# The last layer in one stage: scan over chunks 0 to 4, then 5 to 7, with the gating of the first five chunks between units of the second part

## What is computed

```
# state-space mixer, u of shape (b, l, d), n = 16 states for every channel
A = -exp(log_A)
dt = softplus(u @ W_dt.T + b_dt + dt_bias)
Bt = (u @ W_B.T + b_B).reshape(b, l, d, n)
Ct = (u @ W_C.T + b_C).reshape(b, l, d, n)
A_bar = exp(dt[..., None] * A)
x_in = (A_bar - 1) / A * Bt * u[..., None]
h_t = A_bar_t * h_(t-1) + x_in_t          # along the sequence
y_t = sum_n(Ct_t * h_t) + D_skip * u_t
x = layernorm(u + y)
# mixture
h = gelu(x @ wg1 + bg1); probs = softmax(h @ wg2 + bg2)[:, :20]
top_vals, top_idx = top_k(probs, 2)
out = sum over the two experts e of top_val * (x @ We[e] + be[e])
x = layernorm(x + out)
```

## Time and profile before

| | us |
|---|---|
| median of 3 runs | 2651.47 |
| the three runs | 2647.59, 2654.21, 2651.47 |
| span of the profiled execution | 2646.7 |
| busy in the span: PE / DVE / ACT / POOL | 2472.2 / 1964.7 / 1382.1 / 1110.7 |
| scan: first to last matmul start | 1610.0 to 2339.4 |
| mixture: first pair's matmul | 2415.0 |

### The profile page before, as it was taken

One profiled execution on the slowest core, in us unless ns is written; L12 is line 12 of the kernel. 1 busy time (PEld: TensorE's weight loads), 2 busy tenths in 40 slices (PEclk: granted clock), 3 DMA queues, 4 the chain that ended last, 5 costly groups with the idle time before them and its releaser, 6 DMA issues. The chain is left out here.

```text
span 2646.7 us, 43896 instructions
## 1 busy us (share of the span) xinstructions
PE 2472.2 (93%) x15059; PEld 1552.6 (59%) x15059; DVE 1964.7 (74%) x4037; ACT 1382.1 (52%) x2469; POOL 1110.7 (42%) x1092
## 2 busy tenths in 40 slices
PE   7999999999999999899999997999999999977992
PEld 4433333333333333467777775888888888855772
DVE  3777777777777774266676657999999999975256
ACT  3466666666666666444455535655555555543320
POOL 3522222222222221110000004999989898944454
PEclk9999999999999999999999998999999999987996
DMA  8633333323333321100000000000000000024785
GB/s 244 174 70 71 82 58 58 58 58 58 58 58 69 70 64 66 54 16 17 16 24 25 9 17 8 13 12 12 12 12 12 12 12 12 4 86 130 238 282 162
DMA packets 109601, 166.41 MB, mean 63 GB/s; under 512 B 15876, under 2 KB 74296, under 8 KB 106232
## 3 DMA queue, kind: packets, MB, share of 16 engines
q1 hardware_dynamic: 99064, 143.24, 21.5%
q0 software_dynamic: 6144, 16.79, 2.0%
q10 hardware_dynamic: 4224, 4.19, 0.5%
HBM read 97.66 MB, written 62.01 MB: 60 GB/s over the span
## 5 line engine op out<-in xcount | busy, mean ns | idle before, releaser
L644 ACT ACTIVATE ssm_in_dt<-att_s 128x512 f32<-128x512 f32 (+3 forms) x1280 | 610.0, 535 | 346.9 <-PE att_s L541 182.7
L733 DVE TENSOR_REDUCE att_partmax<-att_s 128x1 f32<-128x512 f32 x768 | 494.3, 686 | 109.8 <-PE att_s L515 66.4
L541 PE MATMUL att_s<-att_qs,att_ks 49*128 49x512 f32 (+3 forms) x1280 | 433.9, 419 | 16.1 <-ACT ssm_in_dt L644 13.8
L515 PE MATMUL att_s<-att_ks,att_qs 49*128 49x512 f32 (+3 forms) x1280 | 434.5, 424 | 4.9 <-DVE att_qs L723 4.7
L541 PEld LDWEIGHTS att_s<-att_qs,att_ks 49*128 49x128 f32 x1280 | 207.4, 185 | 380.3 <-ACT ssm_in_dt L644 307.6
L1797 POOL TENSOR_TENSOR ssm_cc<-ssm_cc,ssm_h 128x512 f32<-128x512 f32 x256 | 334.9, 1308 | 75.7 <-DVE ssm_h L1858 73.8
L432 POOL TENSOR_SCALAR_AFFINE_SELECT ssm_in_dt<-ssm_in_dt 128x256 f32<-128x256 f32 x256 | 104.6, 409 | 621.5 <-ACT ssm_in_dt L644 562.8
L584 PE MATMUL att_o_ps<-ssm_in_dt,att_vst 128*32 128x512 f32 (+3 forms) x2560 | 340.6, 542 | 5.3 <-ACT ssm_in_dt L644 5.3
L1812 POOL TENSOR_TENSOR ssm_out_z<-ssm_out_z,ssm_cc 128x512 f32<-128x512 f32 x256 | 340.4, 1330 | 0.1
L1737 ACT ACTIVATE ssm_cc<-ssm_c_ps,ssm_cur 128x512 f32<-128x512 f32 x256 | 199.0, 777 | 211.8 <-PE ssm_c_ps L1686 211.5
L736 DVE CUSTOM_DVE_ANT_0 att_hid<-att_s,att_hidden 128x512 bf16<-128x512 f32 (+3 forms) x512 | 238.8, 487 | 94.6 <-PE att_s L515 93.7
(11 more groups left out here) (324 smaller groups left out, 4183.7 us busy)
## 6 DMA issues: line engine op xcount, KB each, us to landing
qk_halves<-ssm_in_dt SPq DMA_DIRECT2D x64, 256.0 KB
moe_sorted<-att_hidden SPq DMA_DIRECT2D x31, 512.0 KB, 9.4
moe_rows<-moe_sorted SPq DMA_DIRECT2D x62, 256.0 KB
moe_answers<-moe_mixed SPq DMA_DIRECT2D x62, 256.0 KB
att_far<-bias_tables SPq DMA_DIRECT2D x96, 136.0 KB, 8.5
att_stage_q<-qk_halves SPq DMA_DIRECT2D x96, 128.0 KB, 4.4
att_stage_k<-qk_halves SPq DMA_DIRECT2D x96, 128.0 KB, 5.9
ssm_raw<-in_w_bc SPq DMA_DIRECT2D x30, 256.0 KB, 2.6
```

The source lines that it names most:

```text
L515: mm = nc.tensor.matmul(s1[:, S1_BANK[at], 0:hi - lo], qs[p % 3][half(b, ROWS), I * P:(I + 1) * P], ks[p % 3][half(b, ROWS), lo:hi], start ...
L541: mm = nc.tensor.matmul(s2[:, turn % RING, 0:hi - lo], ks[p % 3][half(b, ROWS), J * P:(J + 1) * P], qs[p % 3][half(b, ROWS), lo:hi], start ...
L644: nc.scalar.activation(prob[:, b, step % 2, x * CH + lo:(x + 1) * CH], s2[:, turn % RING, 0:CH - lo], ACT.Exp, scale=1.0 / HD).then_inc(s2 ...
L733: nc.vector.tensor_reduce(most, piece, AX, ALU.max).then_inc(s1_read, 1)
```

## The change

Both stages become one, `phase_scan`; `phase_mixture` is empty. (The first layer's stage only writes its step sizes chunk by chunk in memory; same instructions.)

1. The units are written out, with no loop on the engines. They run over 32 blocks (n, m) for chunks 0 to 4 (160 units, part one), then over the 32 blocks again for chunks 5 to 7 (96 units, part two). The state at the end of chunk 4 is kept for each block (`carry`), since chunk 5 goes on from it.
2. The rounded weights are made once, in part one, every 5 units. SyncE stores them to DRAM (`scan_halves`, 512 KB a block) and loads them back in part two, one block for 3 units. VectorE's remainder now reads the raw weights from a copy in PSUM.
3. `hi` and `lo` hold 5 chunks; chunks 5 to 7 are rounded over 0 to 2 at the end of part one.
4. PSUM: 3 banks of decays instead of 2, 2 for B instead of 4, 2 for C, and one spare bank, through which all the gating of chunks 0 to 4 goes.
5. The gating of chunks 0 to 4 is put between units of part two at fixed unit numbers: turn c starts at unit 160 + 1 + 7c. Normalising and copying out of transposes move from VectorE to ScalarE for these chunks. GpSimd's 16 scatters of group 0 stand at every second unit from unit 213 to 243.
6. The experts' weights are loaded in part two, over `u` and `dt` of chunks 0 to 4.
7. After the last unit come the pairs at once; `turn_z`, `turn_x`, `hide` and `logits` of chunks 5 to 7 stand among pairs 0 to 14, `count(2)` at pair 18 (before: 14), the exponentials of group 2 at pair 17 (before: 11). The 24 scatters of group 1 follow GpSimd's last unit.

```diff
+PART_CHUNKS = ((0, 1, 2, 3, 4), (5, 6, 7))
...
+def gate(turn):
+
+    return SPLIT + 1 + 7 * turn
...
-            with eng.Fori(0, N - 1) as n:
-                for m in range(KT):
-                    eng.wait_ge(w_ready, KT * n + m + 1)
-                    eng.dma_start(raw[:, m], t.w_bc[ds(n + 1, 1), m].rearrange("a p k c -> (a p) k c")).then_inc(raw_loaded[m], 16)
...
+            def load_halves(b):
+                if b < KT:
+                    eng.wait_ge(halves_stored[b], 16 * N)
+                    eng.wait_ge(c_ready, SPLIT - (KT - 1 - b) * HELD)
+                else:
+                    eng.wait_ge(c_ready, first_unit(b - 1, 1))
+                eng.dma_start(halves[b % KT][:].rearrange("p a k c -> p (a k c)").bitcast(F32), t.halves_bc[b]).then_inc(halves_loaded[b % KT], 16)
...
+                for out_ps, read, ready, ring, col in ((b_ps[:, g % B_RING], b_read, b_ready, B_RING, slice(0, P)),
+                                                       (c_ps[:, g % C_RING], c_read, c_ready, C_RING, slice(P, 2 * P))):
+                    after(eng, read, g - ring + 1)
...
+            for g in range(UNITS):
+                states(g)
+                for c in range(HELD):
+                    for s in range(2):
+                        if g == gate(c) + s:
+                            turn_z(c, s)
+                    for k in range(KT):
+                        if g == gate(c + 2) + 2 + k:
+                            turn_x(c, k)
+                    if g == gate(c + 2) + 4:
+                        hide(c)
+                    if g == gate(c + 3) + 6:
+                        logits(c)
+                if g == gate(6) + 5:
+                    count(0)
+                if g == gate(9) + 5:
+                    count(1)
...
+                nc.scalar.copy(spare.rearrange("p (k c) -> p k c", k=KT), src).then_inc(raw_copied, 1)
...
+                    if g == gate(c + 1):
+                        spread(c)
+                    for j in range(TPC):
+                        if g == gate(c + 1) + (2, 3, 4, 6)[j]:
+                            normalise(c, j)
...
+            for g in range(UNITS):
+                if g + 1 < UNITS:
+                    multiply(g + 1)
+                add(g)
+                for n in range(GROUP_TILES[0]):
+                    for k in range(2):
+                        if g == gate(7) + 3 + 4 * n + 2 * k:
+                            scatter(0, n, k)
...
+                nc.vector.tensor_tensor(halves[m][:, 1], spare.rearrange("p (k c) -> p k c", k=KT), halves[m][:, 0].bitcast(F32),
+                                        ALU.subtract).then_inc(w_ready, 1)
```

More of the change, by code:

```diff
@@ L1003, in tokens @@
         def tokens(c):
-            return dt[:, :, c * CH:(c + 1) * CH]
+            return steps[:, c]
         def expn_at(c):
@@ L1955, with unit, last_unit @@
 STORE_AT = [COMBINED[TPC * q + TPC + 1] + 2 for q in range(EARLY - 1)]
-def phase_mixture(nc, t):
+BLOCKS = N * KT
+PART_CHUNKS = ((0, 1, 2, 3, 4), (5, 6, 7))
+HELD = len(PART_CHUNKS[0])
+SPLIT = BLOCKS * HELD
+UNITS = BLOCKS * NCH
+def unit(g):
+    part = 0 if g < SPLIT else 1
+    chunks = PART_CHUNKS[part]
+    block, at = divmod(g - SPLIT * part, len(chunks))
+    return block // KT, block % KT, chunks[at], block, part, at
+def last_unit(ch):
+    part = 0 if ch in PART_CHUNKS[0] else 1
+    chunks = PART_CHUNKS[part]
+    return SPLIT * part + (BLOCKS - 1) * len(chunks) + chunks.index(ch)
@@ new lines, in decayed, with scan @@
+            def decayed(g):
+                eng.wait_ge(a_ready, g + 1)
+                eng.wait_ge(b_read, g + 1)
+                nc.vector.scalar_tensor_tensor(out=inp[:, g % 2], in0=a_ps[:, g % A_RING], scalar=1.0, in1=inp[:, g % 2],
+                                               op0=ALU.subtract, op1=ALU.mult).then_inc(inp_ready, 1)
+            def scan(g):
+                n, m, ch, b = unit(g)[0:4]
+                after(eng, multiplied, g - H_RING + 1)
+                kept = len([x for x in range(max(0, g - H_RING + 1)) if unit(x)[2] == HELD - 1])
+                if 0 < kept and unit(g - H_RING)[2] == HELD - 1:
+                    eng.wait_ge(carried, kept)
+                if g == SPLIT:
+                    eng.wait_ge(carried, BLOCKS)
+                eng.wait_ge(inp_ready, g + 1)
+                if ch % (S // CH) == 0:
+                    begin = 0.0
+                elif ch == HELD:
+                    begin = carry[:, b:b + 1]
+                else:
+                    begin = h[:, (g - 1) % H_RING, CH - 1:CH]
+                nc.vector.tensor_tensor_scan(h[:, g % H_RING], a_ps[:, g % A_RING], inp[:, g % 2], begin, ALU.mult, ALU.add).then_inc(h_ready, 1)
@@ L2414, in means, with moments, variance @@
+            def moments(c, s):
+                eng.wait_ge(z_copied, 2 * c + s + 1)
+                for j in (2 * s, 2 * s + 1):
+                    ins = nc.vector.bn_stats(stats[:, j], x3[:, TPC * c + j])
+                step.go(ins)
+            def variance(c):
+                step.wait()
+                for j in range(TPC):
+                    ins = nc.vector.bn_aggr(mv[:, TPC * c + j], stats[:, j])
                 ins.then_inc(var_ready, 1)
-            def normalise(c):
+                eng.wait_ge(var_ready, c + 1)
@@ L2528, in _ @@
[L2528 to L2540 removed]
+            pre = t.last_pre
+            step(nc.vector.memset(one[:], 1.0))
+            round_w(0)
+            round_lo(0)
+            nc.vector.scalar_tensor_tensor(out=t.last_expn, in0=pre, scalar=-1.0, in1=pre, op0=ALU.mult, op1=ALU.min).then_inc(last_abs, 1)
@@ L2545, in _ @@
+            whole_normalise(7)
             read_x(7)
-            choose(2)
-            settle(2)
+            read_logits(6)
+            read_logits(7)
+            shift(2)
+            share(2)
+            for q in range(3):
+                largest(2, q)
+            for q in range(3):
+                whose(2, q)
+            chosen(2)
+            joined(2)
+            spots(2)
+            places(2)
+            passes(2)
             list_tiles(2)
```

1254 lines of the change are left out of this document (656 added, 598 removed).

## The result

| | before | changed |
|---|---|---|
| median (8 runs each) | 2649.81 us | 2660.82 us |
| lowest to highest | 2640.92 to 2654.21 | 2659.49 to 2668.29 |
| ratio, 95% interval | | 1.0048 [1.0038, 1.0059] |
| span of the profiled execution | 2646.7 | 2658.8 |

What follows compares the result with a forecast made beforehand. TensorE was taken to bound scan and pairs, with a latency-bound 75 us stretch between. Terms -68 + 26 + 13 - 6 + 2 + 3 + 8 gave -22 us, a median of 2629 us; 8 in 10 within 2603 to 2656.

Steps and rivals of the forecast that it cites:

- Pairs: +8: Pairs' stage: transposes of chunks 5 to 7, waits for chunk 5's chain and for count(2) add 8 us.
- The stretch before the pairs, -68: Between the scan's last matmul and the first pair: 75.5 us shrink to a 7 us wait for GpSimd, gaining 68.
- Part one: Scan of chunks 0 to 4: units stay at 2.80 us, VectorE's remainders fit under TensorE, cost 0.
- Start, -6: First seven units, 32.1 us before: three of six remainders go and the softplus moves behind, 6 us less.
- Part two, 295 to 312 us forecast: Scan of chunks 5 to 7 with the gating between its units: 295 to 312 us long instead of 269.
- the small waits: TensorE's small waits on the gating chain in part two, such as logits behind group 0's places: 3 us more.
- +38: The whole scan, both parts with the start: forecast to take 38 us longer than before.
- The +13: Part two: VectorE's added operations wait 0.6 us each for GpSimd, costing 13 us, between 0 and 33.
- D: Part two: stored weights land late, from 8.4 us on each microsecond costs up to 30 us; slower; chance 10%.
- C: Gating turns in part two: ScalarE becomes the bound through table loads of twice 1.28 us, +10, 2639 us; chance 7%.
- B: Part two: VectorE becomes the bound, each added operation waiting for a whole GpSimd one, +33, 2649 us; chance 12%.
- A: Part two: VectorE's waits for GpSimd fall into its spare time, 13 and 3 unpaid, 2613 us; chance 22%.

Runs made afterwards that it cites:

- c3_after: The changed kernel, unaltered, run again on a chip without the stall: 2621.7 us against 2631.6 for the kernel before, ratio 0.9964.
- e12_before_burst: The kernel before with group 1's scatters no longer waiting for the pairs, on a chip without stalls: ratio 1.0003 to the kernel before.
- e12b_before_burst: The kernel before with the same unpacing of group 1's scatters, on a chip that stalls: 2657.3 against 2644.9 us, ratio 1.0056.

## Why the prediction was wrong

*The failing step is "Pairs: +8".* It priced the transposes among the pairs, the chain of chunk 5 and the count, and gave nothing to the 24 scatters of group 1, which the change lets go without pacing. The description of the change had the sentence; the sum had no term for it, and none of the five rivals was this one. On a chip that stalls the missing term is +31: 223.0 us unpaced against 192.0 paced, on one chip. The paced value is 6 us above the 185.8 of before, where my +8 put it. The rest of the step holds: 6.2 us of waiting at the count (forecast 7).

*Even where nothing stalls, the forecast is missed:* the changed kernel is 10 us faster there, not 22 (c3_after, 2621.7 against 2631.6). No profile of the kernel before is from such a chip, but e12_before_burst takes its time there (1.0003). Against that profile the scan is 39.5 us longer (forecast 38), the gap 60.2 us shorter (71.4 to 11.2; forecast 68), and the pairs' stage 10.3 longer (172.8 to 183.1; forecast 8). So there the step on the gap is the one that is short, since the kernel before loses less in its gap.

*The stretch before the pairs, -68:* measured -64. TensorE waits 8.5 us for GpSimd, whose last addition ends 13 us behind TensorE (forecast 11 less what it gives back). Nothing rested on this wait but an order in a list: with the transposes two pairs later 1.9 us remain.

*Part one:* units take 2.73 us, and the two B banks suffice. The forecast said 2.80, since the kernel before does; over part one that is 11 us gained and not forecast. The remainder with one operand in PSUM takes 680 ns instead of 1692, as taken.

The two rows, DVE's group from 1650 to 2050 and the issues of the changed kernel:

```profile
L2358 DVE TENSOR_TENSOR ssm_halves<-ssm_ps,ssm_halves 128x512 fp32r<-128x512 f32 x29 | 19.7, 680 | 0.0
```

```profile
ssm_halves<-scan_halves SPq DMA_DIRECT2D x32, 512.0 KB, 3.4
```

*Start, -6:* the first seven units take 26.7 us instead of 32.1, -5.4.

*Part two, 295 to 312 us forecast, 324.4 measured.* At 2.73 us the 96 units are 262 us. The groups of the gating's matmuls sum to 30 us (26 forecast), TensorE waits 27. For VectorE, input, count and logits together, it waits 14 (13 forecast); for ScalarE's copies of transposes 12.7, where the small waits had 3. That leaves 5 us, which I put down to matmuls at a lower granted clock (0.97 over the part). So part two is 11 us above my terms, part one 11 below, and the scan's +39 against +38 is right by luck.

The +13 in it is a slip by its own terms: 136 less 121 less 3 is 12. The 14 us measured do not confirm how it was made up either. It had 42 added operations wait 0.6 us each for GpSimd, 25 us. The moments take no longer than before, 414 ns against 412. Some steps of the choice do, like the last two rows below, which took 366 and 176 ns on average before. By such means, all steps of choosing and placing the two groups together take some 15 us more (rows of part two, 2050 to 2379):

```profile
L2450 DVE BATCH_NORM_STATS2 moe_stats<-ssm_out_z 128x6 f32<-128x256 f32 x20 | 7.4, 414 | 0.0
...
L2492 DVE TENSOR_TENSOR moe_pr<-moe_pr,moe_red 128x160 f32<-128x160 f32 (+1 forms) x2 | 4.1, 2040 | 0.1
...
L2517 DVE CAST moe_topf<-moe_topi 128x16 f32<-128x16 uint32 (+1 forms) x2 | 3.2, 1580 | 0.0
```

*The rivals.* D: the stored weights land in 3.4 us (issues by line: count, KB, median us), and no wait of TensorE for them is listed. (Its limit of 9.6 us for "slower than before" is a slip too: 8.4 us and 22 shared out over 30 loads make 9.1.) C: the table load's successor starts 1.29 us behind it (2402.07 to 2403.36 in the changed kernel's timeline), as in the earlier trace rows. The load itself starts as the copy ahead of it ends (2401.47 and 0.58 long). The Trainium skill (ScalarE: Activation LUTs, "What ACT_TABLE_LOAD costs") puts a switch at 2.66 us, 1380 ns of it a drain; by these rows that drain shows on neither side of the load, and the measurement decides. B: VectorE bounds part two where the groups are chosen, not all of it. A: the waits it hoped to see covered were paid.

*The chances* were too sure for another reason too: the sign depends on the chip. The changed kernel takes 0.9964 of the time before on one and 1.0048 on another, and none of my cases had that in it.

## What to carry over

When a change moves a step past a queue, list every wait that the step loses as well as those it gains: a pace in the old code is a term of the sum. Indirect transfers in a long unbroken row on GpSimd's queue are worth pacing even where they fit between other work; on the chips with the stall that gave 29 us here, and on the others nothing (183.1 us of pairs' stage without it, 182.6 with it). An experiment that contradicts another is first repeated beside its reference on one chip.

## What the hardware showed beyond that

- While GpSimd issues indirect DMAs in a row, ScalarE takes TensorE's results late on some chips: 3.7 and 24.9 us behind the matmul for pairs 2 and 3, 14.8 for pair 4 (whose copy stands behind pair 3's), then 0.04 again for pair 5, once the row has ended. A quarter of the bytes changed nothing. VectorE is not likely to be the cause: it worked 5.3 of the 40.7 us, and the scatters kept their 1.27 us. The Trainium skill (SBUF — State Buffer, "SBUF: two separate sides") warns of another thing, that a VectorE instruction in a two-port mode keeps GpSimd from writing its descriptors; by that the scatters would be late, and no run here shows it. That the signal is late is shown by the events above. Whether TensorE itself finished late, since its ends are modelled, and what holds the signal back, stays open.
- The events show it far more widely than the one stall. Counted over all twenty profiles, 2050 to 2600 us, in stretches of 10 us, for TensorE, ScalarE and VectorE: on the chips that stall, 1834 of 3229 signals have their event within 0.1 us where three or more indirect DMAs start in the stretch, 3723 of 3765 where one or two do or some did in the stretch before, and all 7966 elsewhere. On the other chips all have it, also where three or more start (2572 of 2572). So the kernel before and the paced kernels are disturbed too on such a chip, in their scatters and their gathers. A missing event is not always a late signal: SyncE issues the store of pair 1 at 2396.03, 0.03 us behind the copy that it waits for, and that copy's event is not in the trace.
- Chips differ in it: two without the stall (the kernel before at 2628 and 2632 us), at least two with it (2645 to 2650). The kernel before has 16 scatters in a row of its own ahead of the pairs, and its gap behind the scan is 75.0 us on a stalling chip against 71.4 on the other (e12b_before_burst, e12_before_burst). The kernel before differs by 13 to 22 us between the kinds of chip. The profiles of the two kinds say where: against e12_before_burst, whose unpaced scatters cost nothing there, its span is 21.1 us longer, 13.0 of them in the pairs' stage (185.8 against 172.8), 3.7 in the gap, and 4.0 ahead of the scan. The first two are where its indirect DMAs run; an edit that takes all of them away was not tried.
- The same matmul at the same granted clock of 1.00 follows its predecessor after 0.227 us in the changed kernel and 0.233 in the one before: 1250 of them take 283.8 us here (first window above). In the kernel before, as many take 291.2:

```profile
1667.70:1958.90 291.20, 291.20 (x1250) 233.92 (x1249) 278.52 (x327) 156.04 (x236) 263.83 (x210) 1.00 0.04 12
```

  One has its units written out, the other loops, other buffers and other strides. Which of these it is was not tried.
